# Blur stage of a four-stage convolution kernel: who takes the channel mean off, and in how many signals

## The reference, cut to what matters

```python
def _gn(v, G=32, eps=1e-05):            # 32 groups of 32 channels: one channel each
    B_, C_, H_, W_ = v.shape            # 8, 32, 128, 128
    g = v.reshape(B_, G, C_ // G, H_, W_)
    m = jnp.mean(g, axis=(2, 3, 4), keepdims=True)
    s = jnp.var(g, axis=(2, 3, 4), keepdims=True)
    return ((g - m) / jnp.sqrt(s + eps)).reshape(v.shape)

def _L0_conv_ref(x, sigma):
    k2d = _gaussian_kernel2d(sigma)     # 11 x 11, an outer product, the same for all channels
    kernel = jnp.broadcast_to(k2d, (CHANNELS, 1, KSIZE, KSIZE))
    return jax.lax.conv_general_dilated(x, kernel, ..., padding 5 on each side, feature_group_count=CHANNELS)

x = x + _L0_conv_ref(_gn(x), L0_conv_sigma)
```

## Time and profile before

| | before |
|---|---|
| median of 3 runs | 3322.46 us |
| the profiled execution | 3321.49 us |
| its span | 3319.5 us, mean granted TensorE clock 0.877 |
| stage blur, first VectorE work on a chunk to last | 76.4 to 300.7 us |
| chunks | 16 |

### The profile page before, as it was taken

The page is one execution under the profiler, slowest core; times in us unless marked ns, Lnnn a source line. Parts: engine busy times, 40 slices in busy tenths (PEclk is TensorE's granted clock), DMA queues, the critical chain, the costliest instruction groups (busy, mean ns, idle before and its releaser), DMA issues. The chain is left out here.

```text
span 3319.5 us, 86457 instructions
## 1 busy us (share of the span) xinstructions
PE 2512.4 (76%) x38569; PEld 1493.1 (45%) x38569; DVE 2113.5 (64%) x2867; ACT 1819.4 (55%) x1855; POOL 1148.1 (35%) x788
## 2 busy tenths in 40 slices
PE   1774639184999953879999955579999095999998
PEld 0664213022777741235555532157776032555555
DVE  5997767763555546547777758355554663777775
ACT  1111737573555545647767747545555482766775
POOL 0221000101555522654454410055553174444442
PEclk7887879586999976979999977789999596999999
DMA  2455030501111144212222241201111712222221
GB/s 62 122 156 161 19 101 1 202 8 28 28 27 33 25 161 166 57 62 80 83 83 86 81 162 73 28 19 33 28 31 28 303 39 52 80 83 84 85 82 61
DMA packets 213122, 257.73 MB, mean 78 GB/s; under 512 B 79188, under 2 KB 141192, under 8 KB 210696
## 3 DMA queue, kind: packets, MB, share of 16 engines
q1 hardware_dynamic: 203528, 218.58, 22.5%
q0 software_dynamic: 9216, 33.56, 2.5%
HBM read 153.52 MB, written 98.57 MB: 76 GB/s over the span
## 5 line engine op out<-in xcount | busy, mean ns | idle before, releaser
L2053 PE MATMUL dense_spread<-dense_cp,kept_spread_yx 32*128 32x512 f32 x2432 | 479.1, 665 | 67.3 <-DVE dense_cp L2212 60.0
L1323 ACT ACTIVATE snake_samp<-snake_s 128x1024 f32<-128x1024 f32 x320 | 321.3, 1024 | 299.5 <-PE snake_s L1253 299.2
L2232 DVE TENSOR_TENSOR dense_hat<-dense_spread,dense_hat 128x1024 f32<-128x1024 f32 x256 | 301.6, 1220 | 246.7 <-PE dense_spread L2053 246.7
L1386 DVE TENSOR_SCALAR snake_hat<-snake_spread 128x1024 f32<-128x1024 f32 x256 | 301.5, 1219 | 205.1 <-PE snake_spread L1231 205.1
L2157 ACT ACTIVATE dense_hat<-dense_spread 128x1024 f32<-128x1024 f32 x256 | 248.8, 1023 | 284.1 <-PE dense_spread L2053 278.0
L1253 PE MATMUL snake_s<-snake_hat,snake_xt 64*64 64x128 f32 x10240 | 337.5, 274 | 19.4 <-ACT snake_samp L1323 19.1
L2177 ACT ACTIVATE dense_samp<-dense_s 128x864 f32<-128x864 f32 (+1 forms) x384 | 299.1, 833 | 78.6 <-PE dense_s L2103 78.5
L2103 PEld LDWEIGHTS dense_s<-dense_hat,dense_xt 64*64 64x64 f32 x11264 | 267.9, 134 | 145.4 <-issue 95.5
L1253 PEld LDWEIGHTS snake_s<-snake_hat,snake_xt 64*64 64x64 f32 x10240 | 284.9, 133 | 86.0 <-issue 42.2
L657 PE MATMUL dcnoff_acc<-dcnoff_low,kept_w_off 128*64 128x512 f32 x384 | 175.0, 611 | 181.9 <-DVE dcnoff_high L647 177.7
L2103 PE MATMUL dense_s<-dense_hat,dense_xt 64*64 64x108 f32 x11264 | 308.9, 257 | 0.5
(11 more groups left out here) (315 smaller groups left out, 4894.7 us busy)
## 6 DMA issues: line engine op xcount, KB each, us to landing
dense_cp<-offs SPq DMA_DIRECT2D x576, 56.0 KB
x<-blur_x SPq DMA_DIRECT2D x16, 1024.0 KB, 5.1
gateconv_xn<-x SPq DMA_DIRECT2D x16, 1024.0 KB, 11.0
pre<-snake_ob SPq DMA_DIRECT2D x32, 512.0 KB, 3.9
dense_xr<-x SPq DMA_DIRECT2D x64, 256.0 KB, 3.1
out<-dense_xr SPq DMA_DIRECT2D x64, 256.0 KB, 2.5
dense_cp<-offs SPq DMA_DIRECT2D x256, 48.0 KB
offs<-dcnoff_cm SPq DMA_DIRECT2D x64, 144.0 KB
```

The source lines that it names most:

```text
L1323: act.activation(samp[u % 2][:, :, i * MS:(i + 1) * MS, :, :].rearrange("p b m t h -> p b (m t h)"), sample_at(u, i)[:, :, :], ACT.Copy).t ...
L1386: ins = dve.tensor_scalar(strided(hat[u % 2][:, 0:1], GUARD + (4 * tau + 2 * half) * SW * SR, [[8, 2], [SW * SR, 2], [SR, SW], [1, 8]]), s ...
L2053: return pe.matmul(bank[:, :], k.spread_yx[r, kind, :], cp[u % 2][r, tile, :], start=True, stop=True)
L2232: dve.tensor_tensor(h, p_hat[pair][:, :, :].rearrange("p t (r x) -> p (t r) x", x=W), h, ALU.mult).then_inc(main_ready, 1)
```

## The change

GpSimd no longer centres. ScalarE does: one activation (Identity, with the negated mean of a channel as its bias, a 128x1 operand) for each channel, 16 in a chunk, in groups of four with one count of `centred` for each group. TensorE waits for a group before each `along_h` in place of once in a chunk. VectorE writes the negated mean (`less`, by tensor_scalar with -1) in place of the mean, and adds it where it subtracted before. For chunk t+1 ScalarE centres group 0 between copy 2 and copy 3 of chunk t, and groups 1 to 3 after copy 3 and ahead of the square root. The first chunk is centred whole ahead of the first square root.

```diff
+            def centre(slot, q):
+                for n in range(4 * q, 4 * q + 4):
+                    ins = act.activation(cen[slot % 2][:, n, :], xs[slot % SLOTS][:, n, :], ACT.Identity, bias=less[slot % 2][:, n:n + 1])
+                ins.then_inc(centred, 1)
+
+            act.wait_ge(less_kept, 1)
+            for q in range(Q):
+                centre(0, q)
             root(0, True)
...
                     act.activation(half[:, q, :], p_half[q % 2][:, :], ACT.Copy).then_inc(half_copied, 1)
+                    if not last and q == 2:
+                        act.wait_ge(less_kept, t + 2)
+                        centre(slot + 1, 0)
                 if not last:
+                    for q in range(1, Q):
+                        centre(slot + 1, q)
                     root(t + 1, False)
...
                 if before >= 2:
-                    dve.wait_ge(centred, t - 1)
-                dve.tensor_copy(mean[slot % 2][:, :], p_stat[:, 0, slot % 2, :]).then_inc(mean_kept, 1)
+                    dve.wait_ge(centred, (t - 1) * Q)
+                dve.tensor_scalar(less[slot % 2][:, :], p_stat[:, 0, slot % 2, :], -1.0, None, ALU.mult).then_inc(less_kept, 1)
...
-                dve.tensor_tensor(d[:, :], mv[slot % 2][:, :, 0], mean[slot % 2][:, :], ALU.subtract).then_inc(spread_step, 1)
+                dve.tensor_tensor(d[:, :], mv[slot % 2][:, :, 0], less[slot % 2][:, :], ALU.add).then_inc(spread_step, 1)
...
                 def along_h(q):
+                    pe.wait_ge(centred, t * Q + q + 1)
...
-                pe.wait_ge(centred, t + 1)
```

More of the change, by code:

```diff
@@ L73, in blur @@
         mv = [s.sb(f"mean_var{i}", [P, NB, 2]) for i in range(2)]
-        mean = [s.sb(f"mean{i}", [P, NB]) for i in range(2)]
+        less = [s.sb(f"less{i}", [P, NB]) for i in range(2)]
         d = s.sb("d", [P, NB])
@@ L106, in blur @@
         mean_ready = s.sem("mean_ready")
-        mean_kept = s.sem("mean_kept")
+        less_kept = s.sem("less_kept")
         spread_step = s.sem("spread_step")
@@ L157, in _ @@
                       allow_small_or_imprecise_dtypes=True).then_inc(iota_done, 1)
[L159 to L166, removed]
         @block.scalar
@@ L240, in spread @@
                 if before >= 2:
-                    dve.wait_ge(centred, t - 1)
-                dve.tensor_copy(mean[slot % 2][:, :], p_stat[:, 0, slot % 2, :]).then_inc(mean_kept, 1)
-                dve.wait_ge(mean_kept, t + 1)
+                    dve.wait_ge(centred, (t - 1) * Q)
+                dve.tensor_scalar(less[slot % 2][:, :], p_stat[:, 0, slot % 2, :], -1.0, None, ALU.mult).then_inc(less_kept, 1)
+                dve.wait_ge(less_kept, t + 1)
                 dve.wait_ge(mv_ready, t + 1)
-                dve.tensor_tensor(d[:, :], mv[slot % 2][:, :, 0], mean[slot % 2][:, :], ALU.subtract).then_inc(spread_step, 1)
+                dve.tensor_tensor(d[:, :], mv[slot % 2][:, :, 0], less[slot % 2][:, :], ALU.add).then_inc(spread_step, 1)
                 dve.wait_ge(spread_step, t * 2 + 1)
```

## The result

| | before | after |
|---|---|---|
| median of 4 runs | 3323.3 us | 3281.95 us (3280.14 to 3285.38) |
| the profiled execution, its span | 3321.49, 3319.5 | 3282.46, 3280.8 |
| last VectorE work of the blur stage ends | 300.66 | 259.66 |
| mean of chunk 1 to mean of chunk 15, for each of 14 | 13.665 | 10.92 |

The ratio after to before is 0.9876, 95% interval 0.9859 to 0.9893. The forecast was 3281.0, faster.

A forecast was written before the change was run, and what follows sets the result against it. VectorE was taken as the bound, stalled behind GpSimd's centring each chunk. Start +0.5, 14 chunks at -2.73 for -38.3, end -2.65: -40.5 us, from 3321.49 to 3281.0; 8-in-10 range 3271 to 3298.

The forecast's parts named there:

- The stall: VectorE's 16-column square waits for GpSimd's centring; without it 0.17 us in place of 3524 ns, -3.30 us a chunk.
- The price of a centring: ScalarE's 128-column activation: 0.40 us for one, 0.29 from start to start, 4.64 for 16 in a chunk.
- A: Centrings on ScalarE only 0.26 us apart, VectorE keeps the bound, 3273 us; chance 0.12.
- B: Short activations on ScalarE don't overlap, 0.40 us each, cycle 12.7 us, time 3309 us; chance 0.09.
- The new wait: VectorE's reciprocal waits about 0.5 us for ScalarE's root, which ends at 5.45 us behind the mean.
- Rival D: TensorE, in pieces with two waits a chunk, stays at the low clock: 15.0 us a chunk, 3340 us; chance 0.03.
- C: TensorE's clock sags in the gaps, w0, h2, w1 partly slow, 4 to 15 us given back, 3285 to 3296; chance 0.12.
- The reason given for the fast rate: TensorE was slow after 2.31 us of idle time, fast after 1.41; with gaps now 1.4 each, fast was expected.
- The start: Chunk 0 centred whole, then table load and first root: root 1.5 us later, mean of chunk 1 taken as +0.5.
- the working's fast case: At the start, the mean of chunk 1 comes at 93.4 us if TensorE's clock rises, against 94.6 if not.
- The other 1.4: By the page, a table switch costs about 2.66 us including a 1.38 drain, making the start another 1.4 later, once.
- The end: From the mean of chunk 15 to the last finish, 15.5 us before, was forecast to shorten by 2.65.

The follow-up runs named there:

- The early root: The changed kernel with the square root of chunk t+1 between centring groups 1 and 2 in place of behind group 3; 3274.69 us, ratio 0.9858.
- the single signal: The changed kernel with one count of centred per chunk, after its 16th activation, and one TensorE wait ahead of h0; 3301.36 us, ratio 0.9938.
- The four pieces: The kernel before, GpSimd centring in four instructions of 4 channels, TensorE waiting for a group ahead of each along_h; 3295.59 us, ratio 0.9923.

## Why the prediction was right

- **The stall goes.** The forecast was -3.30 a chunk; the square fell from 3524 to 175 ns, 3.35, and putting GpSimd's instruction back returned the time to the ratio 1.0001. The mechanism was read rightly from the common end of the two instructions.
- **The price of a centring.** Forecast 0.40 us for one and 0.29 from start to start. Measured 389 ns, and (3.60 - 0.39)/11 = 0.292. Rivals A and B fall.
- **The new wait.** Forecast about 0.5 us of the reciprocal for the root; its idle time is 0.72, of which 0.15 stand behind every finish, so 0.57. The root came when it was forecast (5.46 us behind the mean, forecast 5.45), the finish ended somewhat sooner than I had it, 4.77 for 4.9. This doesn't change the sum, which goes through ScalarE: 10.76 forecast and measured in the straight part, 10.93 and 10.92 over the 14. The early root, at 10.18 us in place of 10.76, shows that this wait was the bound.
- **TensorE.** Idle times forecast 1.4 and 1.4, measured 1.20 and 1.21; granted clock 1.00 in the middle of the stage. Rival D didn't come, and C in one chunk alone: at 180.59 TensorE had idled 1.64 us for the row mean, the next two groups ran at the low level (x8 in 1.86 and 1.91), and the chunk took 11.25 us. That C was near is shown by the single signal, too: with 2.35 us of idle time the low level came back in every chunk and half of the gain was lost. The reason given for the fast rate, the length of the gaps, is weaker than it was put. With no centring, gaps of 2.26 to 2.60 us mostly left the full level, so the length of one gap doesn't decide alone; the forecast of the clock came true with its reason only in part shown.
- **The start** was the largest miss: +0.5 forecast from mean to mean, -0.2 measured. The working gave 93.4 for the mean if the clock rose and 94.6 if not, and I took a value between them. TensorE was back at the full level by w1 (x8 in 1.06 from 92.47), and the mean came 11.76 behind the first: counted from the 81.70 before, 93.46, the working's fast case. The step that failed is the value between the two. The reciprocal came 1.5 us later than before behind the first mean, as forecast. The other 1.4 of the page "ScalarE: Activation LUTs" (Trainium skill) didn't show: the load starts 0.01 behind the last centring, and the root 0.02 behind the load.
- **The end**: -2.65 forecast, 15.5 to 12.9 measured, -2.6.
- **The sum**: -40.5 forecast; -41.35 from median to median. In the profiled executions the stage gave -41.0: -38.4 for the 14 chunks, -0.2 at the start, -2.6 at the end, and +0.2 as the first mean came later. There 2.3 came back in stages that the change doesn't touch, within what these vary from run to run. That the forecast lies within 1 us of the median is therefore in part luck: the start's 0.7 and the other stages' 2.3 went opposite ways.

## What to carry to other kernels

A very small operation that takes microseconds, and ends with another engine's instruction without reading its output, is a sign of two engines that want the same thing; look whose instruction ends with it, and move, shorten or split that one. When work moves to an engine with room, what it costs is its place in that engine's order, not its length: 4.7 us of centring a chunk cost 0.6, and nothing once the square root stood ahead of half of it. Count the signals that TensorE waits for by the idle time that they leave. With two gaps of 1.2 us a chunk the clock stayed up, but for one chunk; with one of 2.35 us, for a single signal, it fell in each. Don't make a rule of the length: without centring, most gaps of that length left it up.

## What the runs showed of the hardware that was not expected

- A tensor_scalar over 16 columns with a single SBUF input took 3.47 us beside GpSimd's instruction, as the operation with two does.
- Between two of GpSimd's instructions that stand back to back, VectorE gets in: 0.91 and 0.96 us for two operations of 0.175 each. The four pieces took 4.03 us where one instruction took 3.61.
- A scalar_tensor_tensor with one input from PSUM and one from SBUF kept its pace beside GpSimd (12 in 3.18 us).
- With the table load off the path, TensorE idled 0.36 in place of 1.79 us at the start and was back at the full clock sooner (h2 in 1.06 in place of 1.72 us). The mean gained only 0.05 us by that.
- After idle gaps of about the same length TensorE's level differed. With no centring ten of twelve gaps of 2.26 to 2.63 us left it at the full level; with the single signal it fell to the low one behind all of 2.34 to 2.43 us. Which other condition decides isn't shown.
